# A fused attention and gated FFN kernel: row broadcast issued ahead of the token transposes, and W_o turned on TensorE

## What is computed

```python
def _L0_attn_ref(x, Wq, Wk, Wv, Wo):
    q, k, v = split_heads(x @ Wq.T), split_heads(x @ Wk.T), split_heads(x @ Wv.T)
    q, k = _rope(q), _rope(k)                      # 16 heads of 32
    scores = einsum('bhqd,bhkd->bhqk', q, k) / sqrt(dk), causal
    ctx = einsum('bhqk,bhkd->bhqd', softmax(scores), v)
    return ctx @ Wo.T
def _L0_ffn_ref(x, w_fc, w_proj):                  # bitlinear: layer norm, ternary weights
    return bitlinear(gelu(bitlinear(x, w_fc)), w_proj)
xn = _layernorm(x)
s = _L0_attn_ref(xn, Wq, Wk, Wv, Wo)
g = _silu(_L0_ffn_ref(xn, w_fc, w_proj))
return x + s * g
```

## Time and profile before

| | |
|---|---|
| median of 3 runs | 1117.88 us (1117.52 to 1117.99) |
| profiled execution, its own time | 1117.88 us |
| span of the profile | 1116.2 us |
| TensorE busy | 1086.2 us, 97% |
| VectorE, ScalarE, GpSimd busy | 77%, 69%, 47% |
| TensorE's share of the chain that ended last | 88% |
| DMA's share of that chain | 3% |

### The profile page before, as it was taken

The page is one execution under the profiler, slowest core; times in us unless marked ns, Lnnn a source line. Parts: engine busy times, 40 slices in busy tenths (PEclk is TensorE's granted clock), DMA queues, the critical chain, the costliest instruction groups (busy, mean ns, idle before and its releaser), DMA issues.

```text
span 1116.2 us, 19950 instructions
## 1 busy us (share of the span) xinstructions
PE 1086.2 (97%) x7404; PEld 595.3 (53%) x7404; DVE 863.6 (77%) x1623; ACT 772.6 (69%) x1478; POOL 520.6 (47%) x915
## 2 busy tenths in 40 slices
PE   4989999999999999999999999999999999999998
PEld 3555754448444574446634475445844467444763
DVE  6987887898748986689766997579874898668964
ACT  4788984489825887269863798448982688727984
POOL 2036352473716636265443745256371663626533
PEclk9999999999999999999999999999999999999999
DMA  9493005940329104381046510493032910446101
GB/s 320 161 99 92 2 3 83 116 96 21 24 57 156 41 2 68 47 124 39 3 67 75 96 39 3 67 110 87 14 35 51 153 40 2 69 52 81 39 14 65
DMA packets 86401, 75.68 MB, mean 68 GB/s; under 512 B 43168, under 2 KB 68128, under 8 KB 85792
## 3 DMA queue, kind: packets, MB, share of 16 engines
q1 hardware_dynamic: 86304, 74.41, 38.5%
HBM read 31.98 MB, written 8.40 MB: 36 GB/s over the span
## 4 chain that ended last, share of the span: by engine, by line
PE 88%; DVE 5%; DMA 3%; ACT 2%; POOL 1%; issue 1%; SPq 0%; DVEq 0%; POOLq 0%
PE banks L450 22%; PE banks L585 20%; PE banks L630 14%; PE banks L564 6%; PE banks L711 6%; PE banks L692 5%; PE banks L467 5%; PE banks L641 4%; PE banks L571 2%; DMA xT<-xh_buf 2%; ACT banks L892 2%; PE banks L421 1%; PE banks L484 1%; DVE mix L1199 1%; DMA v_sb<-in_L_attn_Wv_dram 1%
## 5 line engine op out<-in xcount | busy, mean ns | idle before, releaser
L892 ACT ACTIVATE banks<-banks,mix,scl 128x384 f32<-128x384 f32 (+2 forms) x384 | 248.1, 648 | 20.9 <-POOL mix L1414 15.7
L1199 DVE TENSOR_REDUCE mix<-banks 128x1 f32<-128x512 f32 (+3 forms) x352 | 216.0, 637 | 27.6 <-PE banks L571 23.3
L585 PE MATMUL banks<-xT,fcT 128*128 128x512 f16 x1024 | 228.6, 380 | 3.2 <-ACT xh_buf L856 2.7
L630 PE MATMUL banks<-proj_ones,arena 128*128 128x256 f16 (+1 forms) x1536 | 213.3, 273 | 0.0
L1405 POOL TENSOR_TENSOR xh_buf<-xh_buf 128x512 f32<-128x512 f32 x120 | 152.4, 1270 | 70.2 <-ACT xh_buf L856 68.8
L915 ACT ACTIVATE arena<-banks,scl 128x1280 f32<-128x1280 f32 x128 | 162.3, 1331 | 29.9 <-PE banks L692 27.1
L450 PE MATMUL banks<-xT,qkT 128*128 128x512 f16 x768 | 168.2, 379 | 0.7 <-DVE arena L1171 0.7
L585 PEld LDWEIGHTS banks<-xT,fcT 128*128 128x128 f16 x1024 | 98.7, 98 | 122.6 <-ACT xh_buf L856 7.2
L630 PEld LDWEIGHTS banks<-proj_ones,arena 128*128 128x128 f16 x1536 | 141.6, 97 | 35.9
L1414 POOL TENSOR_SCALAR mix<-mix,scl 128x1 f32<-128x1 f32 (+1 forms) x288 | 77.2, 268 | 173.5 <-DVE mix L1199 172.2
L861 ACT ACTIVATE banks<-banks,scl 128x512 f32<-128x512 f32 x128 | 84.7, 662 | 76.4 <-PE banks L585 75.2
(11 more groups left out here) (165 smaller groups left out, 1418.3 us busy)
## 6 DMA issues: line engine op xcount, KB each, us to landing
stacks<-xh_buf SPq DMA_DIRECT2D x96, 128.0 KB, 5.2
stacks<-split_buf SPq DMA_DIRECT2D x96, 128.0 KB, 7.4
out_dram<-arena SPq DMA_DIRECT2D x32, 256.0 KB, 2.0
xr_buf<-in_L_attn_x_dram SPq DMA_DIRECT2D x7, 1024.0 KB, 11.1
resid<-in_L_attn_x_dram SPq DMA_DIRECT2D x28, 256.0 KB, 4.3
stacks<-in_L_ffn_w_fc_dram SPq DMA_DIRECT2D x1, 4096.0 KB, 26.8
arena<-in_L_ffn_w_proj_dram SPq DMA_DIRECT2D x1, 4096.0 KB, 15.0
mix<-norm_row SPq DMA_DIRECT2D x8, 256.0 KB, 4.5
```

The costliest lines, as they stand in the source:

```text
L585: mm = pe.matmul(banks[:, UP_BANKS[f % NUB], :], fcT[:, c, f * P:(f + 1) * P], xT[:, part, c, :], start=(c == 0 and part == 0), stop=(c == ...
L630: mm = pe.matmul(banks[:, DOWN_BANKS[h % 3], 0:cols.stop - cols.start], hid[:, part, f, t * P:(t + 1) * P], proj_ones[:, f, cols], start=( ...
L892: mm = nc.scalar.activation(block, block, ACT.Exp, scale=col(EXP_SCALE), bias=exp_bias[:, i, h0 + k:h0 + k + 1], accum_out=row_sum[:, i, h ...
L1199: nc.vector.tensor_reduce(row_max[:, i, h0:h0 + n], scores_of(r), AX_X, ALU.max).then_inc(max_ready, 1)
```

## The change

It has three parts.

1. In `body` of SyncE, `spread_norms(b + 1)` moves ahead of `turn_tokens(b + 1)`, in passes 0 to 6. `rope_rows(b + 1)` on VectorE moves from the end of the pass to behind `finish_context(2)`.
2. W_o is loaded into `xh_buf` (`xhat`) at the start of pass 1, once all four token transposes have landed, and no more in pass 0 into `split_buf`. Who next writes `xh_buf` waits for the four units.
3. W_o is turned on TensorE: four groups of eight f16 transposes between the Q and K matmuls of pass 1, each kept by a copy of ScalarE. The spreading of the largest magnitude moves ahead of pair 0. The four DMA transposes and the semaphore `wo_dma` go.

```diff
@@ buffers
-                    v_sb[:], split_buf[:].rearrange("p a b t -> p (a b t)").bitcast(F32).rearrange("p (c d) -> p c d", c=ND)]
+                    v_sb[:], xhat]
+        OUT_TURNS_AFTER_QK = [[], ou[0:1], ou[1:2], ou[2:3], ou[3:4], [], [], []]
+        OUT_KEPT_BEFORE_ROPE = [ou[0:1], ou[1:3], ou[3:4], []]
@@ SyncE, body
                     if b == 1:
-                        for k, u in enumerate(ou):
-                            sp.wait_ge(w_unit_ready, u + 1)
-                            sp.dma_start(voT[:, 1, :, :, k * P:(k + 1) * P].rearrange("p s c n -> p (s c) n"),
-                                         ring(u).rearrange("p s d -> p (s d)"), transpose=True).then_inc(wo_dma, 16)
+                        for s in xT_dma:
+                            sp.wait_ge(s, 16)
+                        load_weight(raw_attn[3], w_o, 3)
...
-                if first:
-                    for s in stack_dma:
-                        sp.wait_ge(s, 96)
-                    load_weight(raw_attn[3], w_o, 3)
...
                     store_norms(b + 1)
+                    spread_norms(b + 1)
                     turn_tokens(b + 1)
-                    spread_norms(b + 1)
@@ TensorE
-                    for k in range(8 if u < n_first else 0):
+                    for k in range(8 if u < n_first or u >= n_first + n_tern else 0):
...
+                if b == 1:
+                    spread_largest(3, 3, 6)
                 for pair in range(4):
...
-                        if b == 1 and (pair, half) == (0, 0):
-                            spread_largest(3, 3, 6)
...
+                        for u in OUT_TURNS_AFTER_QK[2 * pair + half] if b == 1 else []:
+                            turn_weights(u, u + 1)
                 if b == 1:
-                    pe.wait_ge(wo_dma, 16 * ND)
+                    pe.wait_ge(w_kept, n_units)
@@ ScalarE
-                    if b == 1 and pair == 2:
-                        act.wait_ge(w_unit_ready, n_units)
+                    for u in OUT_KEPT_BEFORE_ROPE[pair] if b == 1 else []:
+                        keep_weights(u)
                     split_rotated(pair)
...
                     act.wait_ge(hid_lo_ready, b * FC + f + 1)
+                    if b == 1 and f == 0:
+                        act.wait_ge(w_unit_ready, n_units)
@@ VectorE
-                    if f == 0 and b == 1:
-                        dve.wait_ge(wo_dma, 16 * ND)
...
                     finish_context(g)
+                    if g == 2 and not last:
+                        rope_rows(b + 1)
...
-                if not last:
-                    rope_rows(b + 1)
```

More of the change, by code:

```diff
@@ L220, in program @@
         tokens_normal, tokens_hi, tokens_split = sem("tokens_normal"), sem("tokens_hi"), sem("tokens_split")
-        wo_dma = sem("wo_dma")
         xT_dma = [sem(f"xT_dma{t}") for t in range(NT)]
```

## The result

The changed kernel takes 1163.87 us (1163.67 to 1164.16), the kernel before 1117.87 (1117.52 to 1117.99): a ratio of 1.0412, with an interval of 1.0394 to 1.0431. The forecast was 1150, the range 1135 to 1168. The profiled execution after has a span of 1162.4 us, where the one before had 1116.2: +46.2.

The account below looks back on a forecast made before the run. TensorE, busy 97% of the span, was taken as the bound. From 1117.9 us, +23.5 for the stall, +6.0 for the clock and +2.4 for W_o gave 1149.8, say 1150 us; range 1135 to 1168.

Parts of the forecast that it names:

- The mechanism: SyncE, ends of passes 0 to 6: token transposes queue behind the broadcast's wait for the column writes, so TensorE waits.
- The stall: TensorE's wait for the first token transpose, passes 0 to 6: 3.9 us each, +23.5 us less the old waits.
- R: Landing time of the norm column writes at the end of pass 3: 569.1, taking 6.1 us behind the last packet.
- The clock: TensorE behind its long waits: half clock costing 1.7 us, counted for half of the seven passes, +6.0 us.
- W_o: Pass 1: turns on TensorE +2.1 us, a 1.0 us wait at the spreading, an old 0.72 gone; together +2.4 us.
- `rope_rows`: VectorE, moved ahead of its last context: waits for the broadcast under cover, gains 0 and costs 0.
- Slow only because transposes are queued behind them: Rival at the wait in `spread_norms`: columns alone land at 564.1, the old waits go, 1116.5 us; chance 0.05.
- The long stall, each time cold: Rival at pass ends: columns land at about 571, wait 5.6 us, clock falls seven times, 1168 us; chance 0.17.
- the clock falling in some passes: The forecast's own case: TensorE's clock falls behind some of the seven waits, 1150 us; chance 0.48.
- Never cold: Rival on TensorE's clock: it never falls behind the seven waits, 1144 us; chance 0.22.
- W_o late: Rival in pass 1: W_o's load takes twice its 5.5 us, 3.6 us over the forecast, 1153 us; chance 0.05.

Follow-up runs that it names:

- e1: The kernel after with SyncE's two calls back in their old order, token transposes ahead of the broadcast: 1134.11 us, ratio 1.0075.
- e3: The kernel before with part 1 alone, broadcast ahead of the token transposes and `rope_rows` early: 1169.96 us, ratio 1.0401.
- e7: The kernel before with the column writes between the token transposes of tiles 1 and 2, broadcast last: 1113.96 us, ratio 0.9966.
- e8: The kernel before with all four token transposes ahead of the column writes, broadcast last: 1119.26 us, ratio 1.0016.
- e6: The kernel after with 24 unused matmuls ahead of TensorE's wait for the first token transpose: 1155.94 us, ratio 1.035.
- e10: The kernel before with the W_o parts of the change alone, run on a third chip: 1127.78 us, ratio 1.0089.
- e2: The kernel before with the W_o parts of the change and nothing else, on the first chip: 1137.94 us, ratio 1.0102.
- e5: The kernel after run again without a change, on a second chip: 1164.98 us, ratio 1.0424.
- e4: The kernel after with 16 unused matmuls ahead of TensorE's wait for the first token transpose: 1168.76 us, ratio 1.0376.
- e12: The kernel after with one of the four norm column writes in passes 0 to 6: 1149.74 us, ratio 1.027.
- e11: The kernel after with norm columns written into one SBUF partition and broadcast from there, from pass 0's end on: 1185.92 us, ratio 1.0592.

## Why the prediction was right, step by step

**The mechanism** was right: the transposes are queued behind SyncE's wait for the columns, in all seven passes, and e1 and e3 show the order to be the loss.

**The stall** was mis-sized: 3.9 us per pass forecast, 4.8 measured (33.5 / 7), so +29.7 us instead of +23.5. The failing number is R. I took 8.75 us from the first column write to the landing, from the 6.1 us behind the last packet in pass 0. Measured in the kernel after it is 8.4 to 11.1 (8.5, 10.4, 8.4, 10.4, 8.8, 9.15, 11.1), mean 9.5. The other steps held: the first transpose lands 5.0 us behind R on average, as taken, and TensorE arrives 9.9 us behind the first column write in six passes and 9.5 in the first. The transpose lands some 1 us behind the broadcast (595.07, the broadcast at 594.05). The Trainium skill ("DMA: Bandwidth & Descriptors", on queues, rings and completion order) says that a semaphore's increment lands only after every earlier write of that DMA engine, and the trace agrees. Of the 5.0 us, 0.4 are the issue and 3.2 to 3.3 the transpose by itself (e7, e8), which leaves some 1.3 for the broadcast in front of it. With 9.5 for 8.75 the working gives 4.6 per pass.

The trace of before had it: by its landings R alternated there too, 8.5, 10.6, 8.9, 10.6, 8.3, 9.8 and 8.9 us, mean 9.4, and the three late passes are the three in which TensorE waited. The prediction took the one figure of pass 0 for all ("Last packet to landing is thus 6.1 us in the one place where the trace shows it"), and at the end of pass 3 this put the landing at 569.1, where it was at about 571.0.

**The clock** was the other mis-sized term: +6.0 forecast ("I count it for half of the seven"), +15.4 measured. It fell behind all seven waits, and cost 2.2 us each time where 1.7 was taken. Here the Trainium skill ("TensorE: Matmul & The Clock Gate", on how its gate bites in real kernels), named with the rival, was the better guide: every one of the waits counted. Its size is shown twice, in the busy time and in e6.

**W_o** came out at +1.9 us in the changed kernel by the trace (forecast 2.4): each group of turns took 0.45 us of TensorE's time where 0.53 was taken, and the new wait only just exceeds the old. Its load landed at 187.03, where 187.0 was forecast, and the reduction began at 190.14, so the load was in time. That the two figures meet is luck: TensorE was free for the V tile at 172.18 instead of 173.35, and the fourth transpose landed 9.3 us behind that instead of 8.2. That W_o's parts cost 2 us behind the stall, and 9.2 (e10) and 13.5 (e2) alone, was not foreseen.

**`rope_rows`** is free in its new place, as said: its wait is followed by 10.30 us of idle time, and e2, without the move, isn't faster than e1.

**The rivals.** "Slow only because transposes are queued behind them" fell: with nothing behind them the columns land as late as before. "The long stall, each time cold" (1168) was nearer to the truth in its clock than the forecast was, and too long in its wait (4.8, not 5.6). The measured 1163.87 lies between the two, 14 us above the forecast and 4 below that rival. So the range held it only because its upper end was taken from this rival, to which I gave 0.17, against 0.48 for the clock falling in some passes. "Never cold" and "W_o late" fell.

## What to carry to other kernels

A wait for a DMA's landing, put into an in-order issue queue, holds up everything behind it; and the 4-byte writes into DRAM landed here some 6 to 8 us after their last packet, with what was queued behind them reporting later still. So put the transfers that the bounding engine is about to need ahead of both, as e7 does, and ask what then comes late (e8). Price a long idle time of TensorE twice, once for itself and once for the half clock behind it: here every one of over 3.1 us was paid twice, and of those between 2 and 3.1 us more than half were.

## What the runs showed of the hardware

- At the ends of passes 0 to 6, 512 writes of four bytes into DRAM landed 8.3 to 11.8 us behind their first issue (before, after, e5 to e10), with transfers queued behind them or, as in the kernel after, with none, and 9.0 to 12.7 on the chip of e1 to e4. In the kernel before the landing is early in one pass and late in the next (8.5, 10.6, 8.9, 10.6, 8.3, 9.8, 8.9); why is open. 128 of the writes still take about 7.2 (e12); into SBUF the 512 take 3.9 to 4.1 (e11).
- A 256 KB broadcast out of a single SBUF partition took 11.7 us, out of DRAM 4.5.
- The clock fell behind each rest of 4.2 to 5.9 us in the kernel after, for stretches of about 3.5 or up to 7 us. Behind pass 0, in all fourteen traces, it fell behind every rest of 3.11 us or more, and behind none of 1.73 or less. Of the thirteen between, it fell behind eight (2.06 twice, 2.08, 2.52, 2.61, 2.73, 2.92 and 3.09) and not behind five (2.25, 2.26, 2.82, 3.04 and 3.09).
- The same rest with the same work around it can do either: the 2.7 us in pass 0 stand in all fourteen traces, and the clock fell behind them in nine and stayed full in e1, e5, e6, e10 and e12.
- One chip ran the kernel before 0.6% slower than the others (1124.42 to 1117.4 and 1118.6). No trace of that kernel was taken there; the traces of other kernels there have later landings of the columns.
